# Graph attention on one Trainium2 core: masks of two source tiles per VectorE instruction, one copy and one add per unit, programs unrolled over heads

## What is computed

```python
def gat_conv(x, W, al, ar, b, src, dst):      # twice, H = 8, D = 32
    h = (x @ W).reshape(N, H, D)
    e = leaky_relu(el[src] + er[dst], 0.2)
    ex = exp(e - m[dst]);  alpha = ex / segment_sum(ex, dst)[dst]
    return elu(segment_sum(alpha[:, :, None] * h[src], dst) + b)

def _gat_head(x, src, dst, Wh, ah, n):        # once, 4 heads, hid = 64
    e = exp(-leaky_relu(alpha_src[src] + alpha_dst[dst], 0.2))
    hp = segment_sum(e[:, None] * h[dst], src) / segment_sum(e, src)[:, None]
    return elu(hp)
```

## Time and profile before

| | value |
|---|---|
| median of 3 runs | 2344.32 us |
| profiled execution | 2345.53 us, its span 2343.7 us |
| share of the span busy | PE 75%, DVE 71%, ACT 59%, POOL 13% |
| mask stages, not split | 433.8 to 776 us and 892.0 to 1235 us, 16 units each |
| mask stage, split | 2028.4 to 2301.8 us, 16 units |
| mean granted TensorE clock | 0.909 of 2.4 GHz |

### The profile page before, as it was taken

One profiled execution on the slowest core, in us unless ns is written; L12 is line 12 of the kernel. 1 busy time (PEld: TensorE's weight loads), 2 busy tenths in 40 slices (PEclk: granted clock), 3 DMA queues, 4 the chain that ended last, 5 costly groups with the idle time before them and its releaser, 6 DMA issues. The chain is left out here.

```text
span 2343.7 us, 65803 instructions
## 1 busy us (share of the span) xinstructions
PE 1751.7 (75%) x21987; PEld 1349.0 (58%) x21987; DVE 1668.3 (71%) x3799; ACT 1378.9 (59%) x2202; POOL 300.0 (13%) x460
## 2 busy tenths in 40 slices
PE   3998865599888336889981399994977995388881
PEld 1333323588888226888881256662546983388881
DVE  6988877899999678999997511113333246799997
ACT  0245763899999238999992411212122352699993
POOL 2465401556100020000000000000000000200000
PEclk9999987799999678999995699997998997699996
DMA  1000000111010001010001110000001010000002
GB/s 60 1 2 2 3 11 2 35 36 34 27 36 25 12 2 40 32 36 36 36 13 51 45 39 0 0 0 6 1 0 37 23 55 10 18 19 25 19 19 89
DMA packets 29718, 54.87 MB, mean 23 GB/s; under 512 B 10222, under 2 KB 20820, under 8 KB 29104
## 3 DMA queue, kind: packets, MB, share of 16 engines
q1 hardware_dynamic: 24608, 43.89, 5.5%
q0 software_dynamic: 4880, 7.80, 1.0%
HBM read 43.19 MB, written 8.49 MB: 22 GB/s over the span
## 5 line engine op out<-in xcount | busy, mean ns | idle before, releaser
L1146 PE MATMUL ps<-R,M 128*128 128x132 f16 (+1 forms) x8640 | 809.4, 221 | 217.4 <-DVE M L1059 112.2
L1015 ACT ACTIVATE Rm<-rows,cB 128x1280 bf16<-128x1280 f32 (+1 forms) x832 | 885.0, 1156 | 35.3 <-DMA rows<-rowd 16.1
L1146 PEld LDWEIGHTS ps<-R,M 128*128 128x128 f16 x8640 | 728.8, 97 | 260.7 <-issue 127.8
L1154 PE MATMUL ps<-HB,C 128*128 128x66 f16 x6400 | 597.0, 193 | 0.0
L1059 DVE TENSOR_TENSOR M<-Rm,C 128x1280 f16<-128x1280 bf16 (+1 forms) x832 | 555.4, 691 | 55.6 <-ACT Rm L1015 48.9
L1154 PEld LDWEIGHTS ps<-HB,C 128*128 128x128 f16 x6400 | 572.4, 97 | 0.0
L1419 PE MATMUL psA<-R,C 128*128 128x512 f16 (+1 forms) x1200 | 253.6, 350 | 96.5 <-POOL ones L1471 41.1
L546 DVE TENSOR_SCALAR ohc<-cells,near 128x1280 f16<-128x1280 f16 x387 | 214.0, 553 | 53.2 <-PE acc L571 47.4
L571 PE MATMUL acc<-ohc,ohl 128*128 128x420 f16 (+1 forms) x1161 | 244.5, 349 | 2.0 <-issue 0.4
L1419 PEld LDWEIGHTS psA<-R,C 128*128 (+1 forms) x1200 | 119.2, 99 | 193.7 <-issue 109.1
L1062 DVE SCALAR_TENSOR_TENSOR M<-rows,cN,C 128x1280 f16<-128x1280 f32 x128 | 197.9, 1546 | 0.0
(11 more groups left out here) (280 smaller groups left out, 2276.8 us busy)
## 6 DMA issues: line engine op xcount, KB each, us to landing
rows<-rowd SPq DMA_DIRECT2D x32, 640.0 KB, 3.8
rows<-rowd SPq DMA_DIRECT2D x16, 320.0 KB, 3.4
xd<-R SPq DMA_DIRECT2D x1, 2560.0 KB, 8.4
xr<-xd SPq DMA_DIRECT2D x20, 128.0 KB, 2.0
xd<-HB SPq DMA_DIRECT2D x1, 2560.0 KB, 9.9
xr<-xd POOLq DMA_DIRECT2D x1, 2560.0 KB, 9.3
R<-in_x SPq DMA_DIRECT2D x1, 2432.0 KB
R<-in_x POOLq DMA_DIRECT2D x1, 2432.0 KB
```

Source lines behind the costliest of these rows:

```text
L1015: a.activation(Rm[:, s % SG, :], rows[:, p % 2, :], ACT.Relu, bias=cB[:, ds(h + s * nh, 1)]).then_inc(s_R, 1)
L1146: m = pe.matmul(region(p % 2, r), lhsT, rhs, start=first, stop=True, skip_group_check=True)
L1154: m = pe.matmul(both[:, :, cw:2 * cw], C[:, s * NP + p * W + r * P:][:, 0:P], VP[:, s, :, ds(h * cw, cw)], start=False, stop=True, skip_gr ...
```

## The change

Masks are made for two source tiles in one DVE instruction. Not split, five tiles are two pairs and one that DVE compares alone; split, the 20 tiles are ten pairs, and `TURNED` becomes whole pairs (2, 3, 6, 7, 12, 13, 16, 17). `Rm` holds two pairs. `M` and `Mn` hold 5 places not split (before 4), and 4 split, which is two pairs (before 5). PE waits once for a pair. The eight PSUM banks become one tensor, and a unit's low halves are copied by one ACT instruction and its high halves added by one DVE instruction, over 12 regions where 10 hold sums (the two spare ones are zeroed once). `q1` goes: the sum is made in `tl`, and ACT's next copy waits for the last read of it. All programs are written out over heads, without loops.

```diff
-                TURNED = [t for t in range(NT) if not split or t % 5 in (1, 3)]
+                TURNED = [t for t in range(NT) if not split or t // 2 % 5 in (1, 3)]
...
-                SG = 5 if split else 4
-                LEAD = 7 if split else 4
+                SG = 4 if split else 5
+                LEAD = 6 if split else 4
+                groups = [(s, s + 1) for s in range(0, NT, 2)] if split else [
+                    g for s in range(0, NT, 5) for g in ((s, s + 1), (s + 2, s + 3), (s + 4,))]
+                pairs = [g for g in groups if len(g) == 2]
+                twice = [g for g in pairs if split and g[0] not in TURNED]
...
-                    Rm = ph.sb("Rm", [P, SG, W], bf16)
+                    Rm = ph.sb("Rm", [P, 4, W], bf16)
...
-                    ps = [[ph.ps(f"ps{b}{j}", [P, 3 * 2 * XW]) for j in range(NB)] for b in range(2)]
+                    ps = ph.ps("ps", [P, 2, NB, 512])
...
+                                before = q * PN + k - 2
+                                if before >= 0:
+                                    a.wait_ge(s_M, before // PN * GN + groups.index(pairs[before % PN]) + 1)
...
+                            a.activation(tl_banks, sums(q % 2, 1), ACT.Copy, scale=1 / LO).then_inc(s_tl, 1)
...
+                            n, last = groups.index(g), q * NT + g[-1]
+                            if last >= SG:
+                                v.wait_ge(s_P, last - SG + 1)
+                            dest = M[:, g[0] % SG:g[0] % SG + len(g), :]
...
+                                v.tensor_tensor(dest, Rm[:, k % 2 * 2:k % 2 * 2 + 2, :], part, ALU.min).then_inc(s_M, 1)
...
+                                v.tensor_tensor(Mn[:, u, :], Cv[:, g[0]:g[0] + 2, p * W:(p + 1) * W], M[:, u, :],
+                                                ALU.subtract).then_inc(s_Mn, 1)
...
+                            for g in some:
+                                mask(q, h, p, g)
+                                if groups.index(g):
+                                    rest_of(q, p, groups[groups.index(g) - 1])
...
+                                v.tensor_tensor(tl_banks, sums(q % 2, 0), tl_banks, ALU.add).then_inc(s_E, 1)
...
+                                if g in twice:
+                                    pe.wait_ge(s_Mn, q * WN + twice.index(g) + 1)
+                                else:
+                                    pe.wait_ge(s_M, q * GN + groups.index(g) + 1)
+                                for s in g:
```

More of the change, by code:

```diff
@@ L37 @@
 SLOPE = 0.2
-MORE_ON_ACT = {(0, 7), (1, 11)}
 EPS = 1e-5
@@ L879, in _ @@
                         if split:
[L880 removed]
+                            turned = V[:, :].rearrange("p (a b h) -> p a b h", b=5, h=2 * nh)[:, :, 1:4:2, :]
                             ch(v.tensor_scalar(turned, turned, -1.0, None, ALU.mult))
@@ L985, in _ @@
                     def _(sp):
[L986 to L1007, removed]
+                        for q, h, p in units:
+                            if q >= 2:
+                                sp.wait_ge(s_M, (q - 1) * GN)
+                            sp.dma_start(rows[:, q % 2, :], row_terms[p, h:h + 1, :].to_broadcast([P, W])
+                                         ).then_inc(s_row[q % 2], 16)
@@ L1009, in _ @@
                     @block.scalar
                     def _(a):
[L1011 to L1034, removed]
+                        def relus(q, h, s0, s1):
+                            a.wait_ge(s_row[q % 2], (q // 2 + 1) * 16)
+                            for k, pair in enumerate(pairs):
+                                if not s0 <= pair[0] < s1:
+                                    continue
+                                before = q * PN + k - 2
+                                if before >= 0:
+                                    a.wait_ge(s_M, before // PN * GN + groups.index(pairs[before % PN]) + 1)
+                                for w, s in enumerate(pair):
+                                    a.activation(Rm[:, k % 2 * 2 + w, :], rows[:, q % 2, :], ACT.Relu,
+                                                 bias=cB[:, h + s * nh:h + s * nh + 1]).then_inc(s_R, 1)
@@ new lines, in evacuate @@
+                        def evacuate(q):
+                            a.wait_ge(s_P, (q + 1) * NT)
+                            a.wait_ge(s_o, q)
+                            a.activation(tl_banks, sums(q % 2, 1), ACT.Copy, scale=1 / LO).then_inc(s_tl, 1)
+                        for q, h, p in units:
+                            relus(q, h, 0, LEAD)
+                            if q:
+                                evacuate(q - 1)
+                            relus(q, h, LEAD, NT)
+                        evacuate(len(units) - 1)
@@ L1051, in steps @@
-                        def steps(h, p, s0, s1, between=()):
-                            between = list(between)
[L1053 to L1065, removed]
+                        for b in range(2):
+                            v.memset(ps[:, b, NB - 1, 2 * XW:6 * XW], 0.0).then_inc(s_E, 1)
@@ L1066, in steps @@
                                 if between:
                                     between.pop(0)()
[L1068 to L1074, removed]
+                            if some[-1] == groups[-1]:
+                                rest_of(q, p, groups[-1])
+                            for stage in between:
+                                stage()
@@ L1113, in unstash @@
-                                ch(v.tensor_copy(room[:, 0:TP, ds(h * cw, dh)], stash[:, :, :]))
-                            stages = [add, scale, both, weight, inverse, mean]
-                            return stages, [unstash] if not split and p == 1 else []
-                        def rest(h, p, before):
-                            stages, last = evacuation(*before) if before else ([], [])
-                            steps(h, p, LEAD, NT, stages + last)
-                        body = parts_in_order(v, steps, rest)
@@ L1123, in _ @@
-                        with v.Fori(1, nh) as h:
-                            ch.begin(h - 1, PARTS * (NB + 5) + (0 if split else 1))
-                            body(h, False)
-                            ch.end(nh - 1)
-                        stages, last = evacuation(nh - 1, PARTS - 1)
-                        for stage in stages + last:
+                                v.wait_ge(s_o, q + 1)
+                                ch(v.tensor_copy(room[:, 0:TP, h * cw:h * cw + dh], stash[:, :, :]))
@@ L1129, in _ @@
+                            return [add, scale, both, weight, inverse, mean] + ([unstash] if not split and p == 1 else [])
+                        early = [g for g in groups if g[0] < LEAD]
+                        for q, h, p in units:
+                            masks(q, h, p, early)
+                            masks(q, h, p, groups[len(early):], evacuation(*units[q - 1]) if q else ())
+                        for stage in evacuation(*units[-1]):
                             stage()
+                        ch.wait()
```

111 lines of the change are left out of this document (51 added, 60 removed).

## The result

The changed kernel takes **2471.35 us** (median of 4 runs, 2467.34 to 2474.48) where the kernel before takes 2345.41 (4 runs, 2344.3 to 2346.53). The ratio is **1.0536, 95% interval 1.0517 to 1.0555**: slower by 126 us, 16 more than the 2455 forecast, and within the range of 2430 to 2490. The profiled execution took 2467.34 us, its span is 2465.3.

The account below looks back on a forecast made before the run. Not split, ACT was taken to bind, a hair ahead of DVE; split, DVE was busiest, ACT close. The split chain's 109 us plus 2 not split made 111 over the 2344.3 median: 2455 us forecast, range 2430 to 2490.

Parts of the forecast that it names:

- The ring decides: Split stage: with a ring two pairs deep, PE and DVE wait for each other, five times a unit; 9.4 us.
- The size of the chain: Split stage: 1.88 us from PE's end of one pair to its start of the next; unit 23.55 against 16.72.
- My lower bound of 23.3: Split stage: shortest unit, in us, with the two transits between PE and DVE at 0.04 each; +105 us.
- The term of the chain: Split stage: sixteen units of 23.55 us against 16.72 add 109 us.
- if the clock leaves 1.00: Split stage: a sign that the forecast is wrong; it expected the granted clock to stay at 1.00.
- the clock falls as well: Split stage, rival: PE's gaps bring the low clock, +308 us instead of +109, 2654 us; chance 7%.
- Loop turns: Mask stages: turns removed by unrolling are already in the 16.72; if fetching long programs stalls as often, 6 us return.
- the turns of the loop had cost ACT something: Stages not split, low end: unit 20.8 us, -8 us.
- Not split: level: Stages not split: ACT waits about 0.25 us, unit 21.05 to 21.15 against 21.04, 0 to 3 us, taken as +2.
- Prices: Instruction pitches in the mask stages: pair of 640 0.73 us, pair of 1280 1.40, addition 0.88, ACT's copy 0.72.
- The rival that a mask of two rows loses its speed: DVE's pair masks run at one column per cycle: +306 and some +215, 2865 us; chance 3%.
- The fast rival: All mask stages: the ring does not bite, split units fall to ACT's 15.7, others to 20.85; -22, 2322 us; chance 4%.

Follow-up runs that it names:

- 3: The changed kernel with M and Mn of the split stage holding three pairs instead of two: 2351.91 us, ratio 1.0025 to the kernel before.
- 4: The changed kernel with a pair's Mn directly behind its own M, the ring still two pairs deep: 2348.99 us, ratio 1.0017 to the kernel before.
- Experiment 7: The changed kernel with 12 unused matmuls on PE before each of the five waits for Mn in a split unit: 2452.38 us, ratio 1.0459.
- 8: The changed kernel with 4 unused matmuls on PE before each of the five waits for Mn in a split unit: 2452.76 us, ratio 1.0457.
- Experiment 9: The kernel before with ACT, DVE and DMA queue programs of the three mask stages written out over heads, without loops: 2330.28 us, ratio 0.9935.
- Experiment 6: The kernel of experiment 5 with later evacuation pieces two groups later in DVE's program in the stages not split: 2314.69 us, ratio 0.9868.
- experiment 5: The changed kernel with three pairs in M, Mn and Rm of the split stage and Mn directly behind its own M: 2323.94 us, ratio 0.9908.
- experiment 1: The changed kernel with the old attention kept for the stages not split, so only the split stage has the change: 2466.85 us, ratio 1.0523.

## Why the prediction was right, point by point

**The ring decides.** Shown, from both sides: the rows of waits have the chain, and either way of opening it takes nearly all of the loss away (3 and 4). The count, five gaps in a unit, is exact. So this step was right, mechanism and number, and not by luck.

**The size of the chain.** The gap was to be 1.88 from stream to stream, which is 1.72 idle behind the last matmul's end; it is 1.66. The row of DVE and PE above gives the parts: 0.03 from PE's end to `M`, 0.75 for `M`, 0.82 for `Mn`, 0.05 to PE's start, where I had 0.11, 0.73, 0.82 and 0.06. The 0.11 is the one mis-sized; I had read it in a row at the low clock (2034.04). A unit at full clock is 23.27 against 23.55 forecast: five times 0.06 is 0.3. My lower bound of 23.3 was also added up wrongly: two transits of 0.04 make the chain 1.79 and the unit 23.1. The term of the chain measures 16 x (23.27 - 16.72) = 105 us where I wrote 109.

**The clock.** This is the step that failed: the forecast has no term for it, and the time lies in the range although one of my own signs of being wrong, "if the clock leaves 1.00", came true. I weighed "the clock falls as well" as a fall for the whole stage, +308 us at 7%, and set it aside by one gap of 1.71 us in a decoder stage with a clock of 1.00. One such gap is no evidence on 80 of them. The clock fell seven times: 4 x 2.54 + 3.15 + 1.5 = 15 us in the profiled execution. Experiment 7 gives 19 us between medians, of which 16 x 0.07 = 1 is that its units are 23.20 and not 23.27. Without the falls the change would take some 2453 (experiments 7 and 8, allowing for that 1 us), 2 us under my 2455; the 16 us by which I missed are the clock's. The median of the change lies 4 us above its profiled execution, and its runs spread over 7 us where 7 and 8 spread over 4; a fall more or less would do that, but I have no profile of the others. The Trainium skill ("TensorE: Matmul & The Clock Gate", HAM oscillation) tells of a kernel in which the clock goes back at every wait between groups of matmuls, waits of 3 to 5 us. The trace agrees that gaps between groups can do it, here gaps of 1.66 to 1.75 us, and not that each does: it fell 7 times in 80 gaps.

**Loop turns.** I took them to be worth 6 us in the split stage and, not split, gave the case that "the turns of the loop had cost ACT something" as the low end, -8. Experiment 9 shows that they cost 6 us there too, and 9 in the split stage. In the split stage the gain sits in the 16.72 from which my sum started, so it changes nothing; what the pairs cost against the same kernel without loops is 16 x (23.27 - 16.15) = 114.

**Not split: level.** Forecast 21.05 to 21.15, measured 21.11, with the wait of ACT at the pair that I named and of the size (0.26 against 0.25). The +2 is 2.4 by the stages, but that it fits is luck. The 21.04 of my row leaves out the longer units at the turns; over the first 14 distances of a stage the kernel before takes 295.2 and 295.3 us and the change 295.6 in both, less than 1 us in all. The rest lies at the stages' edges, where I had put nothing: the first copy comes 1.25 us later, behind 20 `Rm` instead of 19, and the end gives only 0.4 us of that back. And the level of the units is made of two terms that cancel: unrolling gives 0.17 a unit, and the wait takes 0.24 back. Experiment 6 removes the wait and shows the gain.

**Prices.** Pair of 640: 0.75 pitch, forecast 0.73. Pair of 1280: 1.40 as forecast. Addition: 0.89 and 0.88. Copy: 0.71 and 0.72. These steps were right. The rival that a mask of two rows loses its speed is out.

**The fast rival.** 2322 us if the ring did not bite. In this kernel it bites; with the rings and the order opened the time is 2323.94, and ACT's 20 `Rm` and one copy do bound the unit. That the totals lie so close is in part luck: the unit is 15.24 where I had 15.7, 7 us less in all, and the other stages gave nothing where I had -6. The 15.7 was too much because 13 of the 20 `Rm` that I read have a pitch of 0.75 us, and in experiment 5 all 20 have 0.73; the loop is not the reason, since experiment 9 has the 0.75 too. The Trainium skill's advice to keep the number of Vector instructions down ("VectorE: DVE Perf Modes", Rules for kernel authors) holds here only behind a ring that is deep enough; with two pairs it came with the 105 us of the chain. Its worth alone was not measured: 16 us lie between experiment 9 (2330.28) and 6 (2314.69), and 6 also has the joined copy, the deeper rings and the other order.

The sum by terms: 105 (chain) + 15 (clock) + 2.4 (not split) = 122, and the two profiled executions differ by 2467.3 - 2345.5 = 121.8. The match is better than the account: the split stage is 3.6 us longer than its 16 units and falls explain (123.2 - 105 - 15), and the rest of the program is 4 us shorter.

## What to carry to other kernels

When instructions are grouped in pairs, count the ring in groups: four places of one are a lead of three tiles, two places of a pair are a lead of one. Then ask, for the instruction that stands behind a wait for the consumer, whether that same consumer waits for it; if so, the engines take turns, and every step of the producer stands in the consumer's time. Two cures cost nothing but memory or order, and either takes nearly all of the loss away; the gain came only with both and with a third pair of `Rm` for the engine in front.

A change that joins three edits can hide its gain: measure each alone. Here the pairs and the written-out programs were worth 31 us together, once the rings, one line of order and two empty stages were put right.

## What the runs showed of the hardware that I had not expected

- With five gaps of 1.66 to 1.75 us in each unit the granted clock fell from 2.4 to 1.2 GHz seven times in 16 units: four times for some 6.8 us, at a price of 2.54 us each, and three times for some 3.4 us, at about 1.5. Six of the seven falls stand at the one gap with only 1.3 us of work between it and the gap before, and so do six of seven in the profile of experiment 1. With gaps of 1.43 us in the same places, and four matmuls that nobody reads in front of them, the clock did not fall once. Why it falls at some of these gaps and not at all is open.
- Loops over heads on ACT, DVE and the DMA queue cost more than the stall at their turn: ACT's unit of the same 16 `Rm` and four copies is 21.04 us in a loop and 20.87 written out, and the split unit between turns 16.25 and 16.14.
- Joining two DVE instructions into one over twice the columns saves little: 0.06 us for two of 1280 columns (1.40 against 2 x 0.73), 0.05 for two of 640 (0.75 against 2 x 0.40). A mask over two rows of `C` keeps the speed of one.
